# Two-layer graph network on one core: edge keys by ScalarE and TensorE, and all lookups in groups of four windows

## What is computed

```python
edge_index = jnp.stack([src, dst])
h = jnp.maximum(_layernorm(x, axis=-1), 0.0)
x = x + _L0_gnn_ref(h, edge_index, ...)   # twice: h + segment_sum(h[src], dst), then a two-layer net
h = jnp.maximum(_layernorm(x, axis=-1), 0.0)
x = x + _L1_gnn_ref(h, edge_index, ...)   # segment_sum(mlp3(h[src]), dst), then mlp3 of both
return x
```

## Time and profile before

| | us |
|---|---|
| median of 3 runs | 943.83 (942.65 to 955.55) |
| the profiled execution: its time | 934.69 |
| the profiled execution: its span | 932.8 |

### The profile page before, as it was taken

The page is one execution under the profiler, slowest core; times in us unless marked ns, Lnnn a source line. Parts: engine busy times, 40 slices in busy tenths (PEclk is TensorE's granted clock), DMA queues, the critical chain, the costliest instruction groups (busy, mean ns, idle before and its releaser), DMA issues.

```text
span 932.8 us, 25206 instructions
## 1 busy us (share of the span) xinstructions
PE 867.8 (93%) x11282; PEld 708.6 (76%) x11282; DVE 692.4 (74%) x655; ACT 478.2 (51%) x571; POOL 402.5 (43%) x280
## 2 busy tenths in 40 slices
PE   0587999989998999899999999999999989999996
PEld 0367999989898999677777677777777857777774
DVE  7879999999999995574665465566544776777773
ACT  2754646654554453464454445545544555555551
POOL 5888888887000000305534675530010234454450
PEclk9979999999999999999999999999999999999998
DMA  3024344444344234414433434444341567878871
GB/s 111 19 87 155 105 152 140 155 128 132 122 142 141 86 127 146 148 61 138 138 105 113 119 113 125 120 137 120 101 135 50 151 207 201 234 232 245 239 215 46
DMA packets 81857, 126.86 MB, mean 136 GB/s; under 512 B 10288, under 2 KB 58544, under 8 KB 81616
## 3 DMA queue, kind: packets, MB, share of 16 engines
q1 hardware_dynamic: 78608, 121.98, 43.3%
q0 software_dynamic: 3136, 3.22, 1.6%
HBM read 84.22 MB, written 40.94 MB: 134 GB/s over the span
## 4 chain that ended last, share of the span: by engine, by line
PE 54%; DVE 3%; ACT 1%; issue 1%; POOL 0%; DVEq 0%; ACTq 0%; POOLq 0%
PE net_ps_hi L1288 15%; PE net_ps_lo L1288 14%; PE net_ps_lo L1305 7%; PE net_ps_hi L1305 7%; PE net_ps_mt L1231 5%; PE net_ps_ft L1231 2%; DVE net_wide L850 1%; PE net_ps_check L1323 1%; ACT net_wide L1127 1%; DVE hT L943 1%; PE net_ps_hi L1231 1%; PE net_ps_mt L1335 0%; PE net_ps_lo L1231 0%; POOL net_wide L896 0%; PE net_ps_mt L1375 0%
## 5 line engine op out<-in xcount | busy, mean ns | idle before, releaser
L1288 PE MATMUL net_ps_hi<-net_wide,net_first 128*128 128x512 f32 (+1 forms) x637 | 248.5, 394 | 1.3 <-POOL net_wide L896 1.3
L1288 PE MATMUL net_ps_lo<-net_wide,net_first 128*128 128x512 f32 (+1 forms) x637 | 240.8, 382 | 0.0
L1127 ACT ACTIVATE net_wide<-net_raw 128x3584 fp32r<-128x3584 uint8 (+1 forms) x64 | 193.6, 3024 | 78.8 <-PE net_ps_lo L1288 44.8
L850 DVE CAST net_wide<-net_raw 128x3584 fp32r<-128x3584 uint8 (+1 forms) x90 | 201.3, 2245 | 43.9 <-PE net_ps_hi L1305 13.3
L606 PE MATMUL build_ps_out<-build_parts_pad,build_cnts 128*128 128x195 bf16 x2401 | 226.0, 253 | 1.1 <-ACT build_cnts L473 1.0
L344 DVE TENSOR_TENSOR build_hot_lo<-build_grid_lo,build_keys_t 128x4096 bf16<-128x4096 bf16 x98 | 220.5, 2283 | 0.0
L606 PEld LDWEIGHTS build_ps_out<-build_parts_pad,build_cnts 128*128 128x128 fp8e4 x2401 | 206.2, 100 | 5.3 <-ACT build_cnts L473 1.1
L473 ACT ACTIVATE build_cnts<-build_ps_cnt 128x980 uint16<-128x980 f32 (+2 forms) x173 | 148.9, 912 | 113.2 <-PE build_ps_cnt L586 110.8
L1288 PEld LDWEIGHTS net_ps_hi<-net_wide,net_first 128*128 128x128 f32 x637 | 119.8, 188 | 31.9 <-issue 7.0
L1288 PEld LDWEIGHTS net_ps_lo<-net_wide,net_first 128*128 128x128 f32 x637 | 119.9, 188 | 24.7 <-issue 2.6
L850 POOL CAST net_wide<-net_raw 128x3584 fp32r<-128x3584 uint8 (+1 forms) x28 | 84.9, 3031 | 106.7 <-PE net_ps_hi L1305 47.5
(11 more groups left out here) (172 smaller groups left out, 705.9 us busy)
## 6 DMA issues: line engine op xcount, KB each, us to landing
net_raw<-edge_counts SPq DMA_DIRECT2D x168, 448.0 KB, 3.9
edge_counts<-build_cnts SPq DMA_DIRECT2D x168, 224.0 KB
xres<-in_x SPq DMA_DIRECT2D x1, 1568.0 KB, 7.2
net_raw<-edge_counts SPq DMA_DIRECT2D x14, 112.0 KB, 2.0
out<-xres SPq DMA_DIRECT2D x12, 128.0 KB, 4.3
build_rows<-in_dst_rows,build_row_i POOLq DMA_INDIRECT x49, 3.7
build_edges<-in_edges,build_start_i POOLq DMA_INDIRECT x49, 4.3
edge_counts<-build_cnts SPq DMA_DIRECT2D x7, 112.0 KB
```

The source lines that it names most:

```text
L850: return issue(expanded[e % WIDE_RING][:, 0:n, :, :].rearrange("p w a d -> p (w a d)"), raw[e % RAW_RING][:, 0:n, :, :].rearrange("p w a d ...
L1127: expand(act, lambda to, x: nc.scalar.activation(to, x, ACT.Identity), e).then_inc(grown["act"], 1)
L1288: last = nc.tensor.matmul(ps[(b + 1) % 2][:, 0:n * P], first[:, c, lo:lo + H], expanded[e % WIDE_RING][:, 0:n, k, :], start=(c == 0), stop ...
```

## The change

- The keys are no longer computed on VectorE. `find_keys` goes. ScalarE takes four bfloat16 numbers of each edge in two steps (`take_bytes`: low byte of the source over 64, high byte times -4, a sign; `take_distances`: node minus destination, times 128), and TensorE's `turn_keys` transposes and adds them up in float32 PSUM, by four matmuls with scaled identities. The sign corrects for bit 7 of the low byte. The ramps are scaled to match.
- On ScalarE, `take_bytes(u + 2)` follows the copy of count step 0 of pair `u`, `take_distances(u + 2)` that of step 1.
- All groups after the first have four windows. The comparisons of a group stand behind count steps 1 and 2 of pair `FIRST_PAIR - 5`, `find_starts` behind the fourth `hot_lo` of the same pair. For group 3 it is steps 0 and 1 of pair 1 and the fourth `hot_lo` of pair 1, for group 4 steps 1 and 2 of pair 2 and the first `hot_lo` of pair 3.
- GpSimd gathers the rows of group `g + 2` behind the edges of group `g`.
- In the opening pair 1's keys come first, turned after count step 3, and pair 2's later; group 3's comparisons move from there to pair 1. `use(0)` waits for the parts of the features seventh by seventh.
- `net` gets the edges in place of the keys, and `tally_keys` works on them with one operation less of its first six. A constant is added.

```diff
-SPANS = [(0, 2), (2, 6), (6, 10), (10, 14), (14, 18)] + [(w, min(w + 2 * STEP, NW)) for w in range(18, NW, 2 * STEP)]
+SPANS = [(0, 2)] + [(w, min(w + STEP, NW)) for w in range(2, NW, STEP)]
...
-    return {4: (1, 2), 5: (3, 0)}.get(g, (FIRST_PAIR[g] - 6 - 2 * (g - 6), 0))
+    return {3: (1, 0), 4: (2, 1)}.get(g, (FIRST_PAIR[g] - 5, 1))
...
-    return {3: (1, 1), 4: (2, 1), 5: (4, 1)}.get(g, (FIRST_PAIR[g] - 5 - 2 * (g - 6), 1))
+    return {3: (1, 3), 4: (3, 0)}.get(g, (FIRST_PAIR[g] - 5, 3))
...
-                    for later in ROWS_BEHIND.get(g, ()):
-                        gather_rows(later, *SPANS[later])
+                    if g + 2 < len(SPANS):
+                        gather_rows(g + 2, *SPANS[g + 2])
...
-                def find_keys(g):
...
+                def take_bytes(u):
+                    g = group_of(u)
+                    to = key_bytes[:, u % BYTE_RING, :, :].rearrange("p k (w e) -> p k w e", e=RUN)
+                    source = edges[:, 2 * u:2 * u + both(u), :, :].bitcast(U8).broadcast_to([P, 2, RUN, 4])
+                    act.wait_ge(edges_in[g], 16 * (SPANS[g][1] - SPANS[g][0]))
+                    nc.scalar.activation(to[:, 0, :, :], source[:, :, :, 0], ACT.Identity, scale=1 / 64)
+                    nc.scalar.activation(to[:, 1, :, :], source[:, :, :, 1], ACT.Identity, scale=-4.0)
+                    nc.scalar.activation(to[:, 2, :, :], source[:, :, :, 0], ACT.Sign, bias=cut[:, 0:1])
+
+                def take_distances(u):
+                    to = key_bytes[:, u % BYTE_RING, 3, :].rearrange("p (w e) -> p w e", e=RUN)
+                    for t in range(2):
+                        w = min(2 * u + t, NW - 1)
+                        last = nc.scalar.activation(to[:, t, :], edges[:, w, :, 1], ACT.Identity, bias=node128[:, w:w + 1],
+                                                    scale=float(-P))
+                    last.then_inc(keyed, 1)
...
                         copy_counts(u, k)
-                        for g in range(4, len(SPANS)):
+                        if 0 < u < NU - 2 and k == 0:
+                            take_bytes(u + 2)
+                        if 0 < u < NU - 2 and k == 1:
+                            take_distances(u + 2)
+                        for g in range(3, len(SPANS)):
                             pair, at = compare_step(g)
-                            if u == pair and 0 <= k - at < STEP:
+                            if u == pair and 0 <= k - at < -(-(SPANS[g][1] - SPANS[g][0]) // 2):
                                 compare_rows(g, 2 * (k - at), 2 * (k - at) + 2)
...
-                    pe.wait_ge(keyed, group_of(u) + 1)
-                    for k in range(2):
-                        last = nc.tensor.transpose(to[:, k, :], keys[:, k, 2 * u:2 * u + 2, :].rearrange("p w e -> p (w e)"),
-                                                   ident_b[:, :])
-                    return last
+                    pe.wait_ge(keyed, u + 1)
+                    low, tile, top, away = (key_bytes[:, u % BYTE_RING, i, :] for i in range(4))
+                    nc.tensor.matmul(to, top, minus_b[:, None, :].broadcast_to([P, 2, P]), start=True, stop=False)
+                    nc.tensor.matmul(to[:, 0, :], low, ident_b[:, :], start=False, stop=False)
+                    nc.tensor.matmul(to[:, 1, :], tile, ident_b[:, :], start=False, stop=False)
+                    return nc.tensor.matmul(to[:, 1, :], away, ident_b[:, :], start=False, stop=True)
```

The opening on ScalarE, cut to the lines that move:

```diff
                 compare_rows(2)
                 round2(1)
                 round0(4)
+                take_bytes(1)
+                take_distances(1)
                 copy_first(2, 4)
+                copy_first_keys(1)
                 round1(2)
...
                 round2(3)
+                copy_first(4, 6)
+                take_bytes(2)
+                take_distances(2)
                 round0(6)
-                copy_first_keys(1)
+                round1(4)
                 copy_first_keys(2)
-                round1(4)
-                compare_rows(3)
-                copy_first(4, 6)
                 round1(5)
```

103 lines of the change are left out of this document (45 added, 58 removed).

## The result

The changed kernel takes 957.02 us (median of 4 runs, 955.56 to 958.06), the kernel before 944.34 us beside it (942.65 to 955.55). The ratio is 1.015, with a 95% interval of 1.0114 to 1.0186: slower by 12.7 us, where 942.0 us, 2 us faster than before, was forecast and 954 was the upper end of the range. That is slower, though by less than 2%. The profiled execution took 956.6 us, its span is 954.8 us.

A forecast was written before the change was run, and what follows sets the result against it. VectorE was taken to set the build's pace; -12.5 (keys) +0.5 (find_starts) +10.0 (waits) +0.1 (opening) +0.5 -1.4 (TensorE at the end) +0.7 (clock) = -2.1 us, from 943.8 to about 942 us, range 932 to 954.

The forecast's parts named there:

- ScalarE's chain: In the build, from ScalarE's first copy of counts through keys and comparisons to find_starts: 5.38 us.
- five activations: ScalarE's work on a pair's keys, 0.63 us for bytes and 0.47 for distances: 1.10 us, bounds 0.45 and 1.95.
- TensorE's own pace: In the build, four matmuls a turn raise it from 12.49 to 12.66 us a pair, just inside VectorE's 12.68.
- Eight waits: VectorE waits for ScalarE's comparisons at find_starts of groups 5 to 12, 1.25 us each: +10.0 us.
- TensorE begins the pair's counts at 1.95: Working of the find_starts wait: times counted from the end of the pair's first hot_lo, read from the trace.
- The opening: Start of the build: pair 2's hot_a at 63.9 us for 63.76 before, bounds 62.3 and 65.3; +0.1 us.
- The fall of the clock at pair 2: When TensorE starts pair 2, half a fall of its clock worth 1.7 us: +0.7 us.
- The second stage: Matmuls with the count table after the build; touched only in a GpSimd tally, no change of length forecast.
- The -0.9 at the end of the build: TensorE's last steps at a slower pace, +0.5 us, and no longer late at pair 20, -1.4 us.
- No wait at find_starts: Rival: ScalarE's five activations hide or TensorE is earlier, so the gain stays whole; 932 us, chance 0.15.
- TensorE's clock falls at each such wait: Rival: a 3.4 us clock fall after each of eight find_starts waits, +13.6 us; 956 us, chance 0.12.
- ScalarE dearer: Rival: 1.95 us for the five activations, +7 us, or late edges in the opening, +2; 946 to 951 us, chance 0.13.

The follow-up runs named there:

- e8: Changed kernel with find_starts one step later on VectorE and 62 of GpSimd's 98 gathers left out; 936.92 us.
- g1: Changed kernel with find_starts one step later and 62 GpSimd iotas in place of 62 gathers left out; 940.29 us, profiled run 928.65.
- e1: Changed kernel with find_starts one step later on VectorE for the groups from the fourth on; 954.88 us, ratio 0.9993.
- f2: Changed kernel, unchanged, run and profiled again on a quiet chip; 937.58 us, ratio 1.0016.
- c1: Kernel before, unchanged, profiled a second time; 977.64 us.
- the second set: Follow-up runs on one chip, on what pauses TensorE; the kernel before ran at 966.68 us there.
- e6: Changed kernel with 62 of GpSimd's 98 gathers left out, find_starts in its place; 941.13 us.
- c2: Changed kernel, unchanged, run again beside other experiments on their chip; 958.17 us, ratio 1.0047.

## Why the prediction was wrong, step by step

**Right: the parts that the change moves.** VectorE is rid of the keys, and a pair without a wait takes 211.17 - 198.49 = 12.68 us. ScalarE's chain took 5.47 us for 5.38 and its five activations 1.17 us for 1.10. The prediction took 1.64 us as what the Trainium skill's page "ScalarE: Activation LUTs" gives for them. That was read too briefly: the same section, "What ACT_TABLE_LOAD costs", says that back-to-back activations overlap by about 93 ns, which for five makes an estimate of 1.17 us, and the trace agrees. The turn has four matmuls for two transposes, and TensorE's own pace is 12.65 to 12.66 us wherever it sets the pace (e8, g1, and e1 after its last gather), as worked out. Eight waits in the eight pairs named. On a quiet chip six of them are 1.23 to 1.24 us for 1.25, in two pairs of 26.77 us for 26.7.

**Wrong: the length of TensorE's counts was taken as fixed.** The step has "TensorE begins the pair's counts at 1.95", ScalarE's first copy at 2.75 "and 2.9 with the longer turn", from one quiet execution. In the profile after, those runs are broken by pauses, and three times slowed by the clock. The text itself had the price: "A TensorE that comes later only makes VectorE wait as much longer". It had no size for the pauses. The eight waits are 25.9 us and not 10.0. Between the two profiles of the changed kernel (after, and f2), the waits differ by 25.9 - 12.3 = 13.6 us, the opening by 69.27 - 67.13 = 2.1 us, and the build by 397.88 - 381.92 = 16.0 us: waits and opening are nearly all of it. Up to the last of the waits, pauses are 14.0 - 5.1 = 8.9 us ("issue" from 100 to 312 us in either profile) and the three falls of the clock 5.2: together the 13.6 us, within half a microsecond.

**Wrong: what the 9 us between the profile of before and its median were.** The profiled run took 934.69 us and the runs shown 942.65 to 955.55. I carried the 9 us over as a constant. They were most likely the sign of a cost that the profiled run happened not to have (the runs shown have no profile), that another run of the same kernel had 43 us of (c1: 977.64), and that the change could make larger or smaller. On the chip of the second set it is 32 us of the kernel before's median (966.68 - 935) and 21 us of the changed one's (958.17 - 937.58); in the result it was 9 and 19. No step and no rival of the prediction named it, and the range had no room for it.

**Mis-sized, against a quiet chip.** Set against f2 (span 938.6, to 932.8 before, +5.8; the medians say +2.4, with an interval around none) the forecast of -2.1 misses for three terms. *The opening*: pair 2's hot_a at 67.13 and not 63.9. ScalarE's copy of pair 1's first counts came at 62.24 for 60.70 before, since TensorE's first third of use(0) took 4.6 us as before and started 1.3 us later: the half clock moved (the clock averages 0.84 from 50 to 60 us, for 0.56) but was back within that third, so I had counted on it for nothing; that copy's chain took 4.9 us for 4.5. Cost +3.2. *The fall of the clock at pair 2*: 0.7 us in the sum, half of 1.7; it lasted some 7 us and made group 5's wait 4.0 us for 1.25. +2.8 for 0.7, so +2.1, less 0.4 for group 12's shorter wait. *The second stage*: 556.7 us for 554.2, with one fall of the clock where it starts and one near 753 us, neither there before; nothing was forecast for it: +2.5. Together that is 7.4 of the 7.9 us between -2.1 and +5.8. The -0.9 at the end of the build held (from the last hot_a to the end 22.56 us, 23.51 before).

**The rivals.** "No wait at find_starts" did not hold: it is there in all three profiles of the changed kernel. "TensorE's clock falls at each such wait" gave 956 us, the nearest of the four to the 957.02 measured, and that is mostly luck. It held in part: in the profile after three of the eight waits have a fall ahead of them, at the price named (1.75 us for 1.7), which makes 5.2 us and not 13.6. And the wait alone doesn't bring it: on the quiet chip, with six waits of TensorE of about 1.26 us and no pauses, the granted clock from 100 to 300 us averages 1.00 (1.00 too in g1, which has neither, and in e1, which has pauses and almost no such waits). "ScalarE dearer" did not hold: its chain was 5.47 us for 5.38.

**What is shown and what isn't.** Shown: without the gathers there are no pauses (e6 beside c2 in one set); with them, some sets have 9 us and more and some none (c2 and f2, the same kernel, both on chip number 8). Argued only: that TensorE's instructions come late while a gather is made or under way; that c1's stall feeds itself. Not settled: what differs between the sets, why a fall of the clock follows some pauses and not others, and what of a gather does it; the two kernels meant to tell that ran on quiet chips.
